# A fused attention and expert kernel: VectorE's dependent instructions interlaced, two small steps moved to TensorE and ScalarE

## The reference, cut to what matters

```
mod = silu(c) @ wmod                       # six rows of 128 per image
h   = layernorm(x) * (1 + ca) + sa
x   = x + ga * attn(h)
h   = layernorm(x) * (1 + cb) + sb
x   = x + gb * experts(h)
```

## Time and profile before

| | |
|---|---|
| median of 3 runs | 310.82 us (307.86 to 311.46) |
| profiled execution | 308.9 us, span 307.0 us, mean granted TensorE clock 0.898 |
| DVE busy | 277.2 us (90%) in 570 instructions |
| PE busy | 257.3 us (84%), ACT busy 229.4 us (75%) |

### The profile page before, as it was taken

How to read it: one execution, slowest core, us unless ns; L and a number is a source line. 1 busy time by engine, 2 the same in 40 slices (tenths; PEclk the granted TensorE clock), 3 DMA queues, 4 the chain that set the end, 5 groups by cost and what they waited for, 6 DMA issues and landing times.

```text
span 307.0 us, 5136 instructions
## 1 busy us (share of the span) xinstructions
PE 257.3 (84%) x1720; PEld 189.1 (62%) x1720; DVE 277.2 (90%) x570; ACT 229.4 (75%) x636; POOL 38.8 (13%) x64
## 2 busy tenths in 40 slices
PE   6970971999489998999699989999899959888995
PEld 3530830874388477857597568747784758475664
DVE  7799988999979899999999999999999999991772
ACT  3585788799868998898869988998679656845301
POOL 6204001200410011002020011002200400001100
PEclk9596697599958999899969997999699989999999
DMA  5630000020002200140005000500003000400001
GB/s 170 206 97 0 2 0 0 0 71 1 1 2 61 96 1 0 36 138 3 0 1 174 0 0 2 168 8 1 0 37 137 2 1 20 155 0 2 26 9 53
DMA packets 12160, 12.91 MB, mean 42 GB/s; under 512 B 1171, under 2 KB 11110, under 8 KB 11366
## 3 DMA queue, kind: packets, MB, share of 16 engines
q1 hardware_dynamic: 11684, 12.18, 12.8%
q10 hardware_dynamic: 450, 0.40, 0.5%
HBM read 10.43 MB, written 2.15 MB: 41 GB/s over the span
## 4 chain that ended last, share of the span: by engine, by line
DVE 50%; PE 22%; issue 14%; ACT 11%; POOL 2%; DVEq 0%; ACTq 0%; POOLq 0%
DVE AT L788 18%; DVE T L751 12%; PE pT L974 4%; DVE hm L849 4%; PE pR L974 3%; PE pY L1054 3%; ACT c L471 2%; DVE x L805 2%; PE pE L1054 2%; ACT xn L391 2%; DVE endw L776 2%; PE pR L951 2%; DVE x L854 1%; ACT hT L414 1%; DVE prodF L764 1%
## 5 line engine op out<-in xcount | busy, mean ns | idle before, releaser
L751 DVE COPY_PREDICATED T<-mask,T 128x672 f32<-128x672 int16 (+11 forms) x54 | 83.3, 1543 | 0.8
L788 DVE TENSOR_TENSOR AT<-T,c 128x2064 f32<-128x2064 f32 x32 | 72.3, 2301 | 0.0
L488 ACT ACTIVATE A<-pT 128x512 f32<-128x512 f32 x64 | 36.1, 599 | 27.6 <-PE pT L974 27.1
L974 PE MATMUL pT<-first,AT 128*128 128x128 f32 x256 | 43.9, 328 | 13.1 <-DVE AT L796 13.0
L1054 PE MATMUL pE<-hm,late 128*128 128x256 f32 x224 | 52.6, 386 | 0.0
L974 PEld LDWEIGHTS pT<-first,AT 128*128 128x128 f32 x256 | 37.3, 173 | 17.2 <-DVE AT L796 15.5
L1054 PEld LDWEIGHTS pE<-hm,late 128*128 128x128 f32 x224 | 41.2, 190 | 6.6
L974 PE MATMUL pR<-first,AT 128*128 128x128 f32 x256 | 40.4, 311 | 0.0
L315 POOL TENSOR_SCALAR ve<-sq 128x4 f32<-128x4 f32 (+1 forms) x18 | 8.8, 487 | 245.8 <-ACT xn L361 202.2
L488 ACT ACTIVATE A<-pR 128x512 f32<-128x512 f32 x64 | 35.8, 611 | 3.7 <-PE pR L974 3.6
L974 PEld LDWEIGHTS pR<-first,AT 128*128 128x128 f32 x256 | 36.0, 165 | 0.0
(11 more groups left out here) (139 smaller groups left out, 370.9 us busy)
## 6 DMA issues: line engine op xcount, KB each, us to landing
mkb<-mask_rows SPq DMA_DIRECT2D x6, 1024.0 KB, 5.4
x<-in_x SPq DMA_DIRECT2D x7, 256.0 KB, 5.6
out<-x SPq DMA_DIRECT2D x7, 256.0 KB, 5.7
late<-in_late SPq DMA_DIRECT2D x1, 584.0 KB, 3.9
mkb<-mask_rows SPq DMA_DIRECT2D x1, 512.0 KB, 3.8
x<-in_x SPq DMA_DIRECT2D x2, 128.0 KB, 3.5
wmod<-in_wmod ACTq DMA_DIRECT2D x1, 256.0 KB, 3.6
out<-x SPq DMA_DIRECT2D x2, 128.0 KB, 3.3
```

The lines of the kernel that those rows point to most:

```text
L488: nc.scalar.activation(A[b][:, m, 2 * j:2 * j + 2, :].rearrange("p h l -> p (h l)"), four_banks(k)[:, :], ACT.Copy).then_inc(a_A, 1)
L751: nc.vector.copy_predicated(rows[:, :, :, j0:j1], spread(mask[:, k, 0:w, j0:j1], [P, w, H, j1 - j0], 2), rows[:, :, :, j0 + (1 << bit):j1 ...
L788: nc.vector.tensor_tensor(AT[:, bt, :, :].rearrange("p h (j r) -> p h j r", r=BLK), spread(T[n % 2][:, bt, 0:H, 0:NB], [P, H, NB, BLK], 3) ...
L974: ins = nc.tensor.transpose(four_banks(k)[:, c0:c0 + P], AT[:, 2 * b + i, 2 * j + a, m * P:(m + 1) * P], ident)
```

## The change

- VectorE's order is interlaced: where an instruction waited for the one directly before it, another step is now put between. The two sums of the ends lie between the first network stages, masked(0) between the third and fourth, residual between the fourth and fifth (it stood behind the fifth), masked(1) between the fifth and sixth; the four spread_out multiplies stand singly with the steps of `ends_of` between them, and the four products, `offset`, `best` and `cells_from` are spread among one another. The copies of the clipped ends (`set_ends`) come later than their multiplies by one or more instructions.
- `hit` is built with 24 columns at once, and `mk` is gone: TensorE's back_mk now multiplies each of the two hit rows with the identity and adds them in PSUM, two matmuls per tile for one transpose.
- `total` of units 0 to 5 leaves VectorE. TensorE's back_out adds x through the identity (two matmuls per tile for one transpose), and ScalarE copies the sum over x, behind mkT in its order. SP's store waits for that copy. Units 6 to 8 keep `total` on VectorE.
- TensorE runs four more matmuls of 512 columns (`warm_up(4, pT[0])`) between back_x2T and back_logits from i = 1 on.

```diff
--- before.py
+++ after.py
-    c["erow"] = np.broadcast_to(np.arange(E, dtype=np.float32), (P, E)).copy()
+    c["erow"] = np.broadcast_to(np.tile(np.arange(E, dtype=np.float32), NP), (P, NP * E)).copy()
...
-        hit = sb("hit", [P, BT, 2, E]); mk = sb("mk", [P, BT, NP * E])
+        hit = sb("hit", [P, BT, 2, NP * E]);
...
             def store(n):
-                sp.wait_ge(v_out, n + 1)
+                if n < LATE - 1:
+                    sp.wait_ge(a_out, n + 1)
+                else:
+                    sp.wait_ge(v_out, n - LATE + 2)
                 sp.dma_start(rows_of("out", n), of_x(n)).then_inc(d_out, 16)
...
+            def total(n):
+                act.wait_ge(t_out, n + 1)
+                nc.scalar.activation(of_x(n), moe_bank(n)[:, 0:tiles(n) * C].rearrange("p (a c) -> p a c", c=C),
+                                     ACT.Copy).then_inc(a_out, 1)
...
                 run(i, -1, back_mk)
+                run(i, -2, total)
                 run(i, 2, norm1)
...
-                nc.vector.tensor_scalar(f[:, 0:w], sums[:, 0:w, 0], FREQ_T / H, FREQ_MID, ALU.mult, ALU.add)
+                nc.vector.tensor_scalar(f[:, 0:w], sums[:, 0:w, 0], FREQ_T / H, FREQ_MID, ALU.mult, ALU.add).then_inc(v_f, 1)
                 nc.vector.scalar_tensor_tensor(lp[:, 0:w], sums[:, 0:w, 1], PHASE / H, lcol[:, 0:w], ALU.mult,
                                                ALU.add).then_inc(v_fp, 1)
+                dve.wait_ge(v_f, n + 1)
+                nc.vector.reciprocal(invf[:, 0:w], f[:, 0:w]).then_inc(v_inv, 1)
                 dve.wait_ge(v_fp, n + 1)
-                nc.vector.reciprocal(invf[:, 0:w], f[:, 0:w]).then_inc(v_inv, 1)
+                nc.vector.tensor_scalar(lpe[:, 0:w, 0], lp[:, 0:w], -1.0, 1.0, ALU.mult, ALU.add)
+                nc.vector.tensor_scalar(lpe[:, 0:w, 1], lp[:, 0:w], 2.0 - L, None, ALU.add).then_inc(v_lpe, 1)
                 dve.wait_ge(v_inv, n + 1)
                 nc.vector.scalar_tensor_tensor(nlf[:, 0:w], lp[:, 0:w], -1.0, invf[:, 0:w], ALU.mult, ALU.mult).then_inc(v_lin, 1)
-
-            def ends_of(n):
-
-                w = tiles(n)
-                nc.vector.tensor_scalar(lpe[:, 0:w, 0], lp[:, 0:w], -1.0, 1.0, ALU.mult, ALU.add)
-                nc.vector.tensor_scalar(lpe[:, 0:w, 1], lp[:, 0:w], 2.0 - L, None, ALU.add).then_inc(v_lpe, 1)
                 nc.vector.tensor_tensor(fe[:, 0:w, :], spread(f[:, 0:w], [P, w, 2 * END], 2), ends[:, 0:w, :],
                                         ALU.mult).then_inc(v_fe, 1)
+
+            def both(n):
+                return fe[:, 0:tiles(n), :].rearrange("p a (e s) -> p a e s", e=2)
+
+            def past_ends(n):
+
+                w = tiles(n)
                 dve.wait_ge(v_lpe, n + 1)
                 dve.wait_ge(v_fe, n + 1)
-                both = fe[:, 0:w, :].rearrange("p a (e s) -> p a e s", e=2)
-                nc.vector.tensor_tensor(both, both,
+                nc.vector.tensor_tensor(both(n), both(n),
                                         spread(lpe[:, 0:w, :], [P, w, 2, END], 3), ALU.add).then_inc(v_pe, 1)
+
+            def ends_of(n):
+
                 dve.wait_ge(v_pe, n + 1)
-                nc.vector.tensor_scalar(kap[:, 0:w, :, :], both, 0.0, 1.0, ALU.max, ALU.min).then_inc(v_kap, 1)
+                nc.vector.tensor_scalar(kap[:, 0:tiles(n), :, :], both(n), 0.0, 1.0, ALU.max, ALU.min).then_inc(v_kap, 1)
...
+            def offset(n):
+
+                w = tiles(n)
                 dve.wait_ge(v_sc, n + 1)
...
+            def cells_from(n):
+
+                w = tiles(n)
                 dve.wait_ge(v_sf, n + 1)
...
+            def product(n, q, far):
+                if q == 0 and not far:
+                    dve.wait_ge(v_kap, n + 1)
+                    dve.wait_ge(a_row, LT * before(n + 1))
+                own = slice(q, tiles(n), LT)
+                prod, count = ((prodN, END), (prodF, FAR))[far]
+                side = (q + far) % 2
+                c0 = SHIFT[q] + (S - count if side else 0)
+                nc.vector.tensor_tensor(
+                    prod[:, own, :, :], T[n % 2][:, own, 0:H, c0:c0 + count],
+                    spread(kap[:, own, side, 0:count], [P, UNITS[n][1], H, count], 2), ALU.mult).then_inc(v_prod, 1)
+            def sum_ends(n, far):
+                w = tiles(n)
+                dve.wait_ge(v_prod, 4 * (n + 1))
+                if n > 0:
+                    dve.wait_ge(v_end, before(n))
+                own, prod = ((slice(0, 4, 3), prodN), (slice(1, 3), prodF))[far]
+                src = prod[:, 0:w, :, :].rearrange("p (b t) h s -> p b t h s", t=LT)
+                nc.vector.tensor_reduce(cells[:, :, own, :], src, AX.X, ALU.add).then_inc(v_endw, 1)
...
+            def spread_out(n, bt):
+                b = bt // LT
+                if bt == 0:
                     dve.wait_ge(v_net, len(STAGES) * (n + 1))
                     dve.wait_ge(a_c, n + 1)
-                if n > 0:
+                if n > 0 and bt % LT == 0:
                     dve.wait_ge(t_A, 8 * (before(n - 1) + min(b, UNITS[n - 1][1] - 1) + 1))
-                for bt in range(2 * b, 2 * b + 2):
-                    nc.vector.tensor_tensor(
-                        AT[:, bt, :, :].rearrange("p h (j r) -> p h j r", r=BLK),
-                        spread(T[n % 2][:, bt, 0:H, 0:NB], [P, H, NB, BLK], 3),
-                        spread(c[:, bt, :].rearrange("p (j r) -> p j r", r=BLK), [P, H, NB, BLK], 1),
-                        ALU.mult).then_inc(v_mult, 1)
-                dve.wait_ge(v_mult, LT * (img + 1))
-                dve.wait_ge(v_endw, n + 1)
+                nc.vector.tensor_tensor(
+                    AT[:, bt, :, :].rearrange("p h (j r) -> p h j r", r=BLK),
+                    spread(T[n % 2][:, bt, 0:H, 0:NB], [P, H, NB, BLK], 3),
+                    spread(c[:, bt, :].rearrange("p (j r) -> p j r", r=BLK), [P, H, NB, BLK], 1),
+                    ALU.mult).then_inc(v_mult, 1)
+            def set_ends(n, b):
+                dve.wait_ge(v_mult, LT * (before(n) + b + 1))
+                dve.wait_ge(v_endw, 2 * (n + 1))
...
+            def best(n):
                 dve.wait_ge(v_lg, n + 1)
-                for bt in range(w):
-                    ins = nc.vector.max(top[:, bt, :], lg[:, bt, :])
-                ins.then_inc(v_top, 1)
-                dve.wait_ge(v_top, n + 1)
-                for bt in range(w):
-                    ins = nc.vector.max_index(topi[:, bt, :], top[:, bt, :], lg[:, bt, :])
-                ins.then_inc(v_topi, 1)
-                dve.wait_ge(v_topi, n + 1)
-                nc.vector.tensor_tensor(hit[:, 0:w, :, :], spread(spread(erow, [P, 2, E], 1), [P, w, 2, E], 1),
-                                        spread(topi[:, 0:w, 0:2], [P, w, 2, E], 3), ALU.is_equal).then_inc(v_hit, 1)
-                dve.wait_ge(v_hit, n + 1)
+                for bt in range(tiles(n)):
+                    nc.vector.max(top[:, bt, :], lg[:, bt, :]).then_inc(v_top, 1)
+                for bt in range(tiles(n)):
+                    dve.wait_ge(v_top, LT * before(n) + bt + 1)
+                    nc.vector.max_index(topi[:, bt, :], top[:, bt, :], lg[:, bt, :]).then_inc(v_topi, 1)
+            def hits(n):
+                w = tiles(n)
+                dve.wait_ge(v_topi, LT * before(n + 1))
                 if n > 0:
                     dve.wait_ge(t_mk, n)
-                nc.vector.tensor_tensor(mk[:, 0:w, :].rearrange("p a (k e) -> p a k e", e=E),
-                                        spread(hit[:, 0:w, 0, :], [P, w, NP, E], 2),
-                                        spread(hit[:, 0:w, 1, :], [P, w, NP, E], 2), ALU.add).then_inc(v_mk, 1)
+                nc.vector.tensor_tensor(hit[:, 0:w, :, :], spread(spread(erow, [P, 2, NP * E], 1), [P, w, 2, NP * E], 1),
+                                        spread(topi[:, 0:w, 0:2], [P, w, 2, NP * E], 3), ALU.is_equal).then_inc(v_hit, 1)
...
-                run(i, 0, network, range(0, 2))
+                run(i, 0, network, range(0, 1))
                 if i == -1:
                     stats1(1)
                     expert_parts()
-                run(i, 0, sum_ends)
-                run(i, 0, network, range(2, 4))
+                run(i, 0, sum_ends, 0)
+                run(i, 0, network, range(1, 2))
+                run(i, 0, sum_ends, 1)
+                run(i, 0, network, range(2, 3))
                 run(i, -2, masked, 0)
+                run(i, 0, network, range(3, 4))
+                run(i, -1, residual)
                 run(i, 0, network, range(4, 5))
-                run(i, -1, residual)
                 second(i, -2, masked, 1)
                 run(i, 0, network, range(5, 6))
                 run(i, 1, line)
+                run(i, 0, spread_out, 0)
+                run(i, 1, past_ends)
+                run(i, 0, spread_out, 1)
                 run(i, 1, ends_of)
-                run(i, 1, products)
-                run(i, 0, spread_out, 0)
+                run(i, 0, set_ends, 0)
```

(31 more changed lines are left out.)

## The result

The changed kernel takes 324.92 us (median; 323.32 to 326.0), the one before 310.85: a ratio of 1.046 (95% interval 1.039 to 1.053), where 302 was forecast. The profiled execution has a span of 321.5 us.

What follows compares the result with a forecast made beforehand. VectorE, busy 32.26 of a 32.84 us pass, was taken as the bound. From the profiled 308.9 us, -2.5 start-up, +1.65 residual, -7.0 four passes, -0.8 end gave 300.2, plus 1.9 to the median 302; range 298 to 312.5.

Steps and rivals of the forecast that it cites:

- What is late next: Waits after the change: residual for the gate, closing a circle back to line, passes of 31.1 us; masks second candidate.
- the circle's 23.8 us: ScalarE's and TensorE's chain from u's start to the end of mid_gate: 25.2 - 1.5 + 0.15 us.
- the sum: The forecast's addition: -2.5 start-up, +1.65 residual, -7.0 four passes, -0.8 last pass and end, together -8.65 us.
- no GpSimd work moves: Statement in the ScalarE part that the change moves no work of GpSimd; no time was put on it.
- back_mk and back_out: TensorE's added matmuls: 0.4 to 0.5 us more for back_mk, 0.43 more for back_out.
- The end: Last pass and end: -1.1 us by fewer stalls, +0.3 for the longer back_mk, together -0.8.
- The clock: TensorE's clock through mid_A: filling the idle hole keeps it full in most passes, 1.5 us less on the chain.
- The interlacing: VectorE: fourteen waits of 0.12 us saved, 1.7 us a pass; with total, mk and hit 2.35, to 30.5.
- They just fit: Masks landing at L + 20, L being line's start, against VectorE's L + 20.2: they would allow a 30.3 us pass.
- Rival 3: Clock falls each time and slow warm-ups delay the logits: chain over 25.5 us, pass 34, total 316 us; chance 0.10.

Runs made afterwards that it cites:

- resid_back: The changed kernel with residual moved back behind the fifth network stage: 316.23 us, 1.023 of the kernel before.
- hit_gap: The changed kernel with one wait more, the third spread_out multiply waiting for the hits directly before it: 316.44 us, 1.023 of the kernel before.
- pool_dve: The changed kernel with GpSimd's small norm steps on VectorE, square root left out, for timing alone: 309.26 us, 0.999 of the kernel before.
- old_mk: The changed kernel with only mk put back on VectorE, with single transposes in back_mk: 305.45 us, 0.986 of the kernel before.
- old_total: The changed kernel with only total put back on VectorE; hits and the 16 matmuls of back_mk stay: 314.35 us, 1.017 of the kernel before.
- old_mk_total: The changed kernel with mk and all totals back on VectorE and single transposes on TensorE: 301.96 us, 0.980 of the kernel before.
- before_warm: The kernel before the change with nothing but the four warm-up matmuls added: 307.6 us, 0.994 of the kernel before.
- cold_resid: The changed kernel with mk and total on VectorE, no warm-up, and residual behind the fifth stage: 312.58 us, 1.013 of the kernel before.
- old_mk_total_resid: The changed kernel with mk and total on VectorE and residual behind the fifth stage: 305.29 us, 0.986 of the kernel before.

## Why the prediction was wrong

**The failed step is "What is late next": the circle's 23.8 us.** Its form held: 0.95 to u, the chain to the gate, 6.36 back to line. After the change that is 0.92 + (177.50 - 149.58 = 27.9) + 6.4 = 35.2, the measured pass; resid_back took off exactly the stage. The measured 27.9 is 4.1 us more than the 23.8 of the sum: 8.34 from u to the first copy of A (7.72 assumed), 10.32 to the second image's first copy (6.6 assumed), 9.26 to the gate (9.48).

- **GpSimd, priced at nothing by "no GpSimd work moves".** It did not move, but VectorE's multiplies moved beside it: the first now follows line directly, where the small steps of the ends stood, and nm beside it lasts 2.05 us instead of 0.20; and the third lost the gap in front of it. It costs 0.71 us before the second norm and 1.8 before the first: pass 35.3 to 33.4 in hit_gap, 32.6 in pool_dve, where VectorE takes on the steps. The sign was in the trace before, in GpSimd's timeline, and I made nothing of it: an nm of four columns that took 2.19 us at 80.16 lay beside VectorE's multiplies (80.00 to 84.52).
- **back_mk and back_out, priced at 0.4 to 0.5 us each.** They grew by 1.3 each: a float32 matmul stands for two records where a transpose stands for one, and I counted calls. It showed before too: the logits' four matmuls are "x8" in the earlier trace rows. old_mk (32.1) and old_total (33.5) carry one each.
- **The end, priced at 0.3 more by back_mk and 1.1 less by fewer stalls.** From the last line to the end it takes 69.2 us, 63.5 before, 62.9 in old_mk and 64.4 in pool_dve, which keeps the long back_mk; so back_mk alone is not the 5.6 us. The granted clock is near 0.50 from 258 to 265 us, through the logits and the first transposes, where it is 1.00 in the other two, and the masks of that unit come 4.3 us late (0.9 and 1.3 there). Why the clock fell is open: old_mk has the same wait of TensorE in front of it, 2.5 us, and keeps 1.00.
- **Where the 14.5 us of the span are** (321.5 for 307.0): 1.3 up to the line at 113.4, 112.1 before (the sum had -0.85 there), 7.6 in the four passes (-7.0), 5.6 from the last line on (-0.8 with the last pass).
- **The clock: right in direction.** It held in every full pass, though not at the end. Its price was too low: 2.6 us a pass in old_mk_total, not 1.5.
- **The interlacing: right as a sum, not as a gain.** VectorE's work fell as worked out, the 0.12 us of a wait is real. But neither part pays alone: the clock alone gives 1.6 us (before_warm, 307.6), the interlacing alone costs 3.4 (cold_resid, 312.6), and both together gain 4.1 (old_mk_total_resid, 305.3), each against the kernel before as timed beside it. cold_resid's passes, which follow the clock, show what comes next once VectorE's work is less: TensorE's chain.
- **Masks.** "They just fit" was wrong by the same terms: mkT ended at 164.4 instead of 161.8, and the masks landed 2.5 us late; but residual would have waited anyway.
- The forecast of 302 was met by another kernel, old_mk_total, which has the forecast's 6.6 us between the copies (6.37, 153.35 to 159.72) and nearly its pass (31.5 for 31.1). That its total agrees to 0.1 us is partly luck, since it does without both moves of work. **Rival 3 named the right mechanism, a chain of over 25.5 us,** but put it down to the clock, with a chance of 0.10; no rival had GpSimd.

The Trainium skill, page "SBUF — State Buffer", section "SBUF: two separate sides", says that VectorE and GpSimd share a port pair as an exclusive lock, taken also by a VectorE instruction with two SBUF inputs against a GpSimd read. The trace agrees with the lock where nm outlasts the first multiply by 0.06 us (152.05 and 151.99), and goes further: ve was held over two multiplies and near in a row, 5.11 us, not until the end of the one that was running. That the ports are what holds it is the skill's account; the runs show that VectorE's stream holds it, and that a gap lets it through. Weighing that page was the step that I left out.

What stays open: why GpSimd sometimes gets through without a gap, where one multiply follows another (nm before, 80.16 to 82.35) or near follows the second (nm in hit_gap, to 162.64), and at other times doesn't (ve, and an nm of 4.86 us at 88.26 in the changed kernel); and how the start-up's last pass grew from 35.3 to 38.7 us. It is 34.3 in pool_dve, so GpSimd has the largest part, but 39.0 in hit_gap, where that nm takes 0.20 us.

## What to carry to other kernels

When the bounding engine is within a few per cent of another (here VectorE with 32.3 us of work in a pass and TensorE with 30.4), list what each other engine does beside every instruction that moves, GpSimd included, even where none of its own code changes. A wait that looks like pure loss may be the slot through which another engine gets its work done. Cutting the bounding engine's work pays only as far as the next chain allows: here it took the clock and the shorter VectorE together. Count records, not calls, when work goes to TensorE in float32; and where 0 and 1 are all there is, bf16 takes a quarter of the time (0.45 us for the 1.8 of back_mk).

## What the runs showed of the hardware

- GpSimd beside VectorE: a tensor_scalar of four columns takes 0.19 to 0.5 us beside small or dependent instructions, 1.4 beside a stage of copy_predicated, until that ends (182.66 to 184.08 in the changed kernel, the stage to 184.06), 5.11 beside two unbroken 2064-column multiplies, 2.62 with a gap between them, 0.40 with a gap before them.
- VectorE: an instruction that waits for the one directly before starts 0.03 us after its end, another 0.09 ahead of it; adding one such wait made the kernel over 2% faster than the changed one (316.4 for 324.9 us; 1.023 for 1.046 of the kernel before).
- TensorE: float32 matmul 2 x 0.11 us for 128 columns, transpose 1 x 0.11, bf16 matmul with 24 columns of weights 1 x 0.055, all at full clock.
